# Attention block: values projected for four pairs of heads at a time, through DRAM, their bias added at the split of the output

## What is computed

```python
hn = (h - mu) * rsqrt(var + 1e-05) * gamma + beta
q = (hn @ Wq + bq).reshape(b, s, 16, 64)
k = (hn @ Wk + bk).reshape(b, s, 16, 64)
v = (hn @ Wv + bv).reshape(b, s, 16, 64)
q, k = _rope(q), _rope(k)
attn = softmax(where(tril, einsum('bihd,bjhd->bhij', q, k) / 8, -inf))
out = einsum('bhij,bjhd->bihd', attn, v).reshape(b, s, 1024)
x = _layernorm(h + out @ Wo + bo + h)
x = _layernorm(x + x + ffn(x))
```

## Time and profile before

| | |
|---|---|
| Time, median of 3 runs | 2310.25 us (2309.42 to 2313.67) |
| Profiled execution | 2305.9 us, span 2304.1 us |
| Granted TensorE clock, mean | 0.973 of full speed |
| Busy: TensorE, VectorE, ScalarE, GpSimd | 2144.3, 1691.7, 958.2, 1435.4 us |
| Attention pairs | from 71.5 us to about 1977 us |
| Transfers | 100.45 MB, 44 GB/s on average |

### The profile page before, as it was taken

The page is one execution under the profiler, slowest core; times in us unless marked ns, Lnnn a source line. Parts: engine busy times, 40 slices in busy tenths (PEclk is TensorE's granted clock), DMA queues, the critical chain, the costliest instruction groups (busy, mean ns, idle before and its releaser), DMA issues.

```text
span 2304.1 us, 43543 instructions
## 1 busy us (share of the span) xinstructions
PE 2144.3 (93%) x15872; PEld 1407.3 (61%) x15872; DVE 1691.7 (73%) x2318; ACT 958.2 (42%) x1301; POOL 1435.4 (62%) x1204
## 2 busy tenths in 40 slices
PE   5779999999999999899999999999999999889997
PEld 4446565556565656455656565556565654789996
DVE  8567878787878787777877777787777775466654
ACT  3334444444434443434444444444344445333433
POOL 2447777777777777566868686878687779200000
PEclk8799999999999999989999999999999999899999
DMA  5100101010101011101111111111111130222200
GB/s 161 63 22 19 46 19 46 21 43 22 42 24 41 24 41 54 48 19 32 33 32 33 32 33 33 33 32 33 33 29 36 29 115 10 96 92 73 100 19 28
DMA packets 79484, 100.45 MB, mean 44 GB/s; under 512 B 13984, under 2 KB 43680, under 8 KB 79008
## 3 DMA queue, kind: packets, MB, share of 16 engines
q1 hardware_dynamic: 79264, 97.60, 14.2%
HBM read 40.93 MB, written 23.07 MB: 28 GB/s over the span
## 4 chain that ended last, share of the span: by engine, by line
PE 73%; DVE 17%; issue 6%; ACT 1%; DMA 1%; SPq 1%; POOL 1%; DVEq 0%; ACTq 0%
PE o_ps L1150 17%; PE m_ps L1098 8%; DVE mpart L748 6%; PE x_ps L1053 6%; PE s_ps L1119 4%; PE x_ps L1055 4%; PE x_ps L1054 4%; PE s_ps L1121 4%; PE s_ps L1125 4%; PE s_ps L1123 4%; PE gu_ps L1053 2%; PE gu_ps L1054 2%; PE gu_ps L1055 2%; PE x_ps L1157 1%; DVE rot L787 1%
## 5 line engine op out<-in xcount | busy, mean ns | idle before, releaser
L474 POOL TENSOR_TENSOR acc<-acc,pt 128x512 f32<-128x512 f32 (+3 forms) x1024 | 1235.4, 1238 | 232.6 <-ACT pt L533 232.0
L748 DVE TENSOR_REDUCE mpart<-m_ps 128x2 f32<-128x1024 f32 (+2 forms) x576 | 625.6, 1086 | 342.1 <-PE m_ps L1098 205.5
L533 ACT ACTIVATE pt<-s_ps 128x1024 f32<-128x1024 f32 (+3 forms) x640 | 545.1, 896 | 561.7 <-PE s_ps L1125 319.5
L1150 PE MATMUL o_ps<-pt,v 128*64 128x512 f32 (+3 forms) x2560 | 555.4, 556 | 0.0
L1098 PE MATMUL m_ps<-qk 64*128 64x512 f32 (+3 forms) x1280 | 285.8, 442 | 102.5 <-DVE mpart L748 85.1
L1098 PEld LDWEIGHTS m_ps<-qk 64*128 64x128 f32 x1280 | 121.8, 186 | 384.0 <-issue 217.3
L1150 PEld LDWEIGHTS o_ps<-pt,v 128*64 128x64 f32 x2560 | 158.5, 139 | 232.5 <-issue 211.4
L469 POOL TENSOR_TENSOR acc<-pt 128x512 f32<-128x512 f32 (+1 forms) x128 | 165.5, 1313 | 200.0 <-ACT pt L533 200.0
L1119 PE MATMUL s_ps<-qk 64*128 64x512 f32 (+3 forms) x1280 | 249.8, 385 | 0.0
L1121 PE MATMUL s_ps<-qk 64*128 64x512 f32 (+3 forms) x1280 | 235.9, 363 | 0.0
L1125 PE MATMUL s_ps<-aux,ones_r 64*128 64x512 f32 (+3 forms) x1280 | 235.8, 362 | 0.0
(11 more groups left out here) (161 smaller groups left out, 3406.7 us busy)
## 6 DMA issues: line engine op xcount, KB each, us to landing
rot<-qr SPq DMA_DIRECT2D x512, 64.0 KB, 2.0
attn<-o_n SPq DMA_DIRECT2D x64, 256.0 KB, 2.1
o_raw<-attn SPq DMA_DIRECT2D x8, 2048.0 KB, 9.0
w_raw<-in_wqkv SPq DMA_DIRECT2D x51, 128.0 KB, 2.6
h_g<-in_h SPq DMA_DIRECT2D x8, 512.0 KB, 3.6
out<-out_g SPq DMA_DIRECT2D x7, 512.0 KB, 2.9
qk_place<-in_h SPq DMA_DIRECT2D x4, 512.0 KB, 5.8
pt<-in_h SPq DMA_DIRECT2D x4, 512.0 KB, 10.6
```

The costliest lines, as they stand in the source:

```text
L474: nc.gpsimd.tensor_tensor(sums, sums, probs, ALU.add).then_inc(summed, 1)
L533: nc.scalar.activation(pt[:, u % SLOTS, :, q0:NB], s_ps[:, two:two + 2, q0:NB], ACT.Exp, scale=SCALE)\
L748: nc.vector.tensor_reduce(dst, m_ps[:, :, 0:w], AX.X, ALU.max, negate=True).then_inc(maxed, 1)
L1150: last = nc.tensor.matmul(o_ps[rows, q0:NB], v[par][:, j, rows], pt[:, u % SLOTS, a, q0:NB], start=(j == 0), stop=(j == n - 1), skip_group ...
```

## The change

The values are no longer made for one pair of heads but for four (512 columns of Wv). One *piece* is a tile of 128 tokens: 6 matmuls with 512 columns into the bank. Four pairs need 16 pieces, and there are four such sets (two for each sequence). The first set is made in the opening; the second in pairs 0 to 3, four pieces in each, at the groups where the V chunks stood; the third, first of the second sequence, in pair 7, 16 pieces at `SWITCH_PLACES`, where a place (g, 1) is behind the weighing and sums of group g; the fourth in pairs 8 to 11, four in each. In pairs 4 to 6 and 12 to 15 none are made.

ScalarE copies a piece to `v_part`, SyncE stores it in `v_far` in DRAM (256 KB), and before each pair SyncE loads that pair's 128 columns into its `v` buffer: tiles 0 to 11 (768 KB) in group 1 of the pair before, tiles 12 to 15 (256 KB) in group 2 of the pair itself, both in runs of 512 bytes. For pair 8 the first load stands in group 14 of pair 7. The weights of four pairs, `wv_hl`, are loaded and split apart from those of Q and K, so the loads of `w_raw` per pair are two and not three.

The bias of the values is added where the attention output is split, from a column per partition. The loops of `each_pair` are written out. `o_n` and `r_b` are gone: the division is in place, and ScalarE's copy of the next `o_ps` waits for the store. The buffers of the last part stand in another order.

```diff
-VALUES = {g: int(x[1]) for g, x in XUSE.items() if x[0] == "V"}
+V_GROUPS = [g for g, x in XUSE.items() if x[0] == "V"]
+
+
+
+SWITCH_PLACES = [(3, 1), (4, 1), (5, 1), (7, 1), (8, 1), (9, 0), (9, 1), (10, 1), (11, 1), (13, 1), (14, 0), (14, 1),
+                 (15, 1), (16, 0), (16, 1), (17, 1)]
+V_PIECES = {it: {} for it in range(2 * PAIRS)}
+for it in range(4):
+    V_PIECES[it] = {(g, 0): (TT + 4 * it + i, 4 * it + i) for i, g in enumerate(V_GROUPS)}
+    V_PIECES[PAIRS + it] = {(g, 0): (3 * TT + 4 * it + i, 4 * it + i) for i, g in enumerate(V_GROUPS)}
+V_PIECES[PAIRS - 1] = {place: (2 * TT + i, i) for i, place in enumerate(SWITCH_PLACES)}
+
+WV_LOAD = {(0, 2): 2, (0, 5): 3, (5, 3): 4, (5, 6): 5, (8, 2): 6, (8, 5): 7}
+WV_SPLIT = {(0, 4): 2, (0, 7): 3, (5, 5): 4, (5, 8): 5, (8, 4): 6, (8, 7): 7}
+
...
-            pair(FIRST, 0, 0, 0, 0)
-            with engine.Fori(0, PAIRS // 2 - 1) as two:
-                pair(MIDDLE, two * 2 + 1, 1, two * 2 + 1, 0)
-                pair(MIDDLE, two * 2 + 2, 0, two * 2 + 2, 0)
-            pair(SWITCH, PAIRS - 1, 1, PAIRS - 1, 0)
-            pair(MIDDLE, PAIRS, 0, 0, 1)
-            with engine.Fori(0, PAIRS // 2 - 1) as two:
-                pair(MIDDLE, two * 2 + (PAIRS + 1), 1, two * 2 + 1, 1)
-                pair(MIDDLE, two * 2 + (PAIRS + 2), 0, two * 2 + 2, 1)
-            pair(LAST, 2 * PAIRS - 1, 1, PAIRS - 1, 1)
+            kinds = {0: FIRST, PAIRS - 1: SWITCH, 2 * PAIRS - 1: LAST}
+            for it in range(2 * PAIRS):
+                pair(kinds.get(it, MIDDLE), it, it % 2, it % PAIRS, it // PAIRS)
...
+            def load_v(it, c0, c1, done):
+
+                here, cols = slice(TG * c0, TG * c1), slice(it % 4 * P, (it % 4 + 1) * P)
+                sp.dma_start(v[it % 2][:, here, :], v_far[it // 4, here, :, cols].rearrange("t p n -> p t n"))\
+                  .then_inc(done, 16)
+
+            def store_v(it, place):
+                if place in V_PIECES[it]:
+                    n, t = V_PIECES[it][place]
+                    sp.wait_ge(v_done, n + 1)
+                    sp.dma_start(v_far[n // TT, t, :, :], v_part[:, :]).then_inc(v_stored, 16)
...
                 n0 = batch * SEQ + blk * NB
-                sp.dma_start(attn[bass.ds(head_rows, P), n0:n0 + NB], o_n[:, :]).then_inc(o_stored, 16)
+                sp.dma_start(attn[bass.ds(head_rows, P), n0:n0 + NB], o_sum[:, :]).then_inc(o_stored, 16)
...
                     if g in PIECE and kind is not LAST:
                         swap_halves(it + 1, *PIECE[g])
+                    store_v(it, (g, 0))
+                    store_v(it, (g, 1))
+                    if kind is SWITCH and g == 14:
+                        sp.wait_ge(v_stored, 16 * v_stored_for(it + 1, 2))
+                        load_v(it + 1, 0, 3, v_in)
+                    if (it, g) in WV_LOAD:
+                        sp.wait_ge(wv_lo, WV_LOAD[it, g])
+                        load_wv(WV_LOAD[it, g], wv_raw[:, :])
+                    if g == 2:
+                        if v_stored_for(it, 3) > 0:
+                            sp.wait_ge(v_stored, 16 * v_stored_for(it, 3))
+                        load_v(it, 3, 4, v_in3)
...
+                    if g == 1 and kind is not LAST:
+                        sp.wait_ge(pv_done, max(it * NG, 1))
+                        if kind is not SWITCH:
+                            if v_stored_for(it + 1, 2) > 0:
+                                sp.wait_ge(v_stored, 16 * v_stored_for(it + 1, 2))
+                            load_v(it + 1, 0, 3, v_in)
...
+                for t in range(TG * c, TG * (c + 1)):
+                    sp.wait_ge(v_done, t + 1)
+                    sp.dma_start(v_far[0, t, :, :], v_parts[t % 4]).then_inc(v_put[t % 4], 16)
...
+                if c == 0:
+                    for done in v_put:
+                        sp.wait_ge(done, 16 * BLOCKS)
+                    load_v(0, 0, 3, v_in)
...
             def evict_o(n, blk):
                 act.wait_ge(pv_done, n * NG + (BLOCK_ENDS[blk] + 1))
-                act.wait_ge(normed, n * BLOCKS + (blk + 1))
+                act.wait_ge(o_stored, (n * BLOCKS + blk) * 16 + 16)
                 nc.scalar.activation(o_sum[:, :], o_ps[:, :], ACT.Copy).then_inc(o_out, 1)
...
+            def evict_v(n, bank, dst):
+                act.wait_ge(v_proj, n + 1)
+                nc.scalar.activation(dst, bank, ACT.Copy).then_inc(v_done, 1)
+
+            def evict_v_first(c):
+                for t in range(TG * c, TG * (c + 1)):
+                    if t >= 4:
+                        act.wait_ge(v_put[t % 4], 16 * (t // 4))
+                    evict_v(t, v_bank[t % 2], v_parts[t % 4])
+
+            def evict_v_piece(it, place):
+                if place in V_PIECES[it]:
+                    n = V_PIECES[it][place][0]
+                    if n > TT:
+                        act.wait_ge(v_stored, 16 * (n - TT))
+                    evict_v(n, x_ps[:, :], v_part[:, :])
...
+                    evict_v_piece(it, (g - 1, 1))
...
-            def values(n, c, par, i):
-                dve.wait_ge(v_proj, n * BLOCKS + (c + 1))
-                if c == 0:
-                    dve.wait_ge(b_in, n * 32 + 32)
-                if c == 0 and i == 2:
-                    dve.wait_ge(pv_done, n * NG - NG)
-                nc.vector.tensor_tensor(v[par][:, TG * c:TG * (c + 1), :],
-                                        v_bank[i].rearrange("p (t n) -> p t n", t=TG),
-                                        b_v[:, par, :].unsqueeze(1).broadcast_to([P, TG, P]), ALU.add)\
-                  .then_inc(v_done, 1)
+            def rest_wv(n, raw):
+                dve.wait_ge(wv_hi, n + 1)
+                nc.vector.tensor_tensor(wv_hl[:, 1, n % KC, :], raw, wv_hl[:, 0, n % KC, :].bitcast(F32),
+                                        ALU.subtract).then_inc(wv_lo, 1)
...
             def divide(n, blk):
                 dve.wait_ge(r_back, n * BLOCKS + (blk + 1))
                 dve.wait_ge(o_out, n * BLOCKS + (blk + 1))
-                dve.wait_ge(o_stored, (n * BLOCKS + blk) * 16 + 16)
-                nc.vector.tensor_tensor(o_n[:, :], o_sum[:, :], r_b[:, :], ALU.mult).then_inc(normed, 1)
+                nc.vector.tensor_tensor(o_sum[:, :], o_sum[:, :], r_t[:, :], ALU.mult).then_inc(normed, 1)
...
-            def project_v(n, c, i):
-                for t in range(TG):
-                    here = slice(NB * c + P * t, NB * c + P * (t + 1))
-                    for k in range(KC):
-                        last = product(v_bank[i][:, t * P:(t + 1) * P], [hn[:, x, k, here] for x in range(2)],
-                                       [w_hl[:, x, k, 2 * P:3 * P] for x in range(2)],
-                                       first=(k == 0), last=(k == KC - 1))
+            def project_v(n, t, bank):
+
+                pe.wait_ge(wv_lo, KC * (n // TT + 1))
+                here = slice(P * t, P * (t + 1))
+                for k in range(KC):
+                    last = product(bank, [hn[:, x, k, here] for x in range(2)], [wv_hl[:, x, k, :] for x in range(2)],
+                                   first=(k == 0), last=(k == KC - 1))
                 last.then_inc(v_proj, 1)
...
                     if j == 0:
-                        pe.wait_ge(v_done, it * BLOCKS + (blk + 1))
+                        if blk == 0:
+                            pe.wait_ge(v_in, 16 * (it + 1))
+                        if blk == BLOCKS - 1:
+                            pe.wait_ge(v_in3, 16 * (it + 1))
...
-                def shared_free(g):
-
-                    for before in range(g - 1, -2, -1):
-                        x = XUSE[before % NG]
-                        n, i = (it if before >= 0 else it - 1), int(x[1])
-                        if x[0] in "QKV" and nxt:
-                            if x[0] == "V":
-                                pe.wait_ge(v_done, n * BLOCKS + (BLOCKS + i + 1))
-                            else:
-                                pe.wait_ge(cos_done, n * (2 * BLOCKS) + (2 * BLOCKS + 2 * i + "QK".index(x[0]) + 1))
+                def shared_free(g, behind):
+
+
+                    for place in range(2 * (NG * it + g) + behind - 1, -1, -1):
+                        n, b, late = place // (2 * NG), place // 2 % NG, place % 2
+                        if (b, late) in V_PIECES[n]:
+                            pe.wait_ge(v_done, V_PIECES[n][b, late][0] + 1)
                             return
-                        if x[0] == "M":
-                            own = n if before % NG < NG - 1 else n + 1
-                            pe.wait_ge(aux_done, own * BLOCKS + (i + 1))
+                        if late and b in SUMMED and (n, b) != (0, 0):
+                            pe.wait_ge(r_turned, (n - 1 if b == 0 else n) * BLOCKS + (SUMMED[b] + 1))
                             return
-                        if x[0] == "R" and (before > 0 or kind is not FIRST):
-                            own = n if before > 0 else n - 1
```

(25 more changed lines are left out.)

## The result

| | before | after |
|---|---|---|
| median | 2310.91 us (4 runs, 2309.42 to 2313.67) | 2294.75 us (4 runs, 2291.1 to 2298.65) |
| profiled execution, its span | 2305.9, 2304.1 us | 2298.65, 2296.9 us |

The ratio after to before is 0.9929 (95% interval 0.991 to 0.9948): faster by 16 us (0.7%), where 60 were forecast, and 4.75 us above the upper end of the range, 2290. The two profiled executions lie 7.25 us apart, since the one of before is 5 us under its median and the one of after is the slowest of its four.

What follows compares the result with a forecast made beforehand. TensorE's own instructions were taken as the bound (busy 93% of the span). Terms -50 - 31.5 - 2 + 2 + 19 + 4 - 8.5 + 7 gave -60 us: 2250 us as a median, range 2220 to 2290.

Steps and rivals of the forecast that it cites:

- I charge 3 us of new waits to a pair without V: Pairs 4 to 6, 12 to 14: 11.3 us of chunks gone, 3 us of TensorE waits added; six times 8.3, 50 less.
- Rival 2: VectorE, coupled with GpSimd, takes over; pairs without V gain 4 us, four-piece pairs 2.5; 2290 us; chance 0.18.
- Rival 1: TensorE stays the only bound; waits charged to relieved pairs and pair 7 vanish; 2223 us; chance 0.13.
- Rival 3: Q0's and K0's half swaps queue behind the value loads, slower than before; 2347 us at 100 GB/s; chance 0.05.
- 4 us for transfers: Value and weight loads ahead of Q0's half swaps delay them: 0.3 us a pair, 4 us more in all.
- Rival 4: Bank x_ps chains pieces everywhere, TensorE waiting for ScalarE's copy or a store; 2281 us; chance 0.06.
- Four-piece pairs: Pairs 1 to 3 and 8 to 11: 4.5 us less each, 31.5 in all; pairs 1 to 3 at 111 to 112.
- Pair 7: Switch of batches, 16 pieces for 4 chunks: 13.7 us of matmuls plus 5 of bank waits, 19 more (12 to 27).
- Splits of the V weights: VectorE's added splits in pairs 5 and 8, beside TensorE: 1 us each, 2 us more.
- The opening and pair 0: Opening: 16 pieces for 4 chunks, half hidden, 7 us more (3 to 14); pair 0: net 2 us less.
- Loops: Pairs 1 to 6 and 9 to 14 written out, no jumps: 8.5 us less (4 to 13).
- Pair 15 and the rest: Pair 15 had no V chunks and has no pieces; eviction, bias, stores and output copy were priced at nothing.

Runs made afterwards that it cites:

- short_rope: Changed kernel with VectorE's sine product, sum and remainder cut from 512 to 32 columns in pairs 4 to 6 and 12 to 14, output wrong: 2241.19 us.
- loops_out: Kernel before, with only the loops over pairs 1 to 6 and 9 to 14 written out: 2304.45 us, ratio 0.997 to before.
- fill6: Changed kernel plus six unread 512-column matmuls at each former V chunk place in pairs 4 to 6 and 12 to 14: 2280.52 us.
- fill24: Changed kernel plus 24 unread 128-column matmuls at each former V chunk place in pairs 4 to 6 and 12 to 14: 2304.51 us.
- two_pairs: Changed kernel with values made for two pairs at a time, eight pieces of two tiles by 256 columns a set: 2280.39 us.
- p7_moved: Changed kernel with pair 7's pieces moved from straight behind K0 and K1, and pair 8's first value load in group 18: 2293.52 us.
- two_spread: Against values made for two pairs at a time: second split-weight buffer, splits in groups 10 and 11, pair 7's row splits in eight halves: 2252.86 us.

## Why the prediction was wrong, step by step

**The step that failed** is "I charge 3 us of new waits to a pair without V". Held against short_rope, the waits cost 11.6 us in pair 13: 6.6 us of idle time and 5.0 us of the matmuls' own time at a lower granted clock. The term stood in the sum as -50 us for six pairs; the six pairs fell by 7.8 us in the traces (-5.4 and -2.4), of which loops_out has 2.3 (350.8 to 348.9 and 348.6 to 348.2), so the chunks gave 5.5, or 0.9 a pair, and what was charged at 3 us came to 10.4 on average. That is 44.5 us too few. Between the two traces the kernel fell by 7.2 us where 60 were forecast, a miss of 52.8; the other terms missed by 8.3 together, by errors of up to 9 us in both directions that follow below. (Between the medians the miss is 44.75 us. That this is nearly the 44.5 of the step is chance, since the execution profiled before lies 5.0 us under its median and the one after 3.9 above.) The bound was wrong too: I put the least gain of such a pair at 4 us, and it was 0.9.

Two readings led there. First, I took "TensorE busy 33.94 of 34 us" as proof that a microsecond of matmuls there is one of the pair. It says only that TensorE doesn't wait; that it had been filled to the point where VectorE comes ready is seen in the order of time, where the maxima start 0.05 us behind the reduction. Second, I compared VectorE's busy share over a block (84 to 88%), while the wait is set between two reductions, where three 512-column operations stand in a row. The sum to make was that of VectorE's instructions between two reductions against TensorE's between the two maxima.

**The clock** was in no term. The earlier trace rows had it: 0.91 in pair 0 and 0.94 in pair 7, where TensorE waits, 0.99 in pair 8, where it hardly does.

**Rival 2** gave 2290, the nearest number, and its sign came: the relieved pairs stayed above 112 us, with TensorE's idle time at the reductions. Its reason holds by half: VectorE does set the length of these pairs, but at single places and together with TensorE's clock, and not by being full. It had pairs with four pieces gain 2.5 us; they gained 4.4 (27.6 us in pairs 1 to 3 and 9 to 11, less 1.1 that loops_out has). And with VectorE alone as the bound fill6 could not have gained. **Rival 1** is excluded by fill24. **Rival 3**: VectorE's whole wait for swapped halves is 7.7 us (8.9 before), where I had said near 9, and a swap lands in 2.0 us as before; so no run shows anything of the 4 us for transfers. **Rival 4**: outside pair 7 TensorE shows no wait for the bank.

**Four-piece pairs**: forecast 111 to 112 us, found 110.9 to 112.4, with 113.5 in pair 9. A piece of pair 2, from its first matmul on:

```profile
407.73 0.50 PE L1147 MATMUL x_ps<-wv_hl,hn 128*128 128x512 f32 x1
408.06 0.39 PE L1148 MATMUL x_ps<-wv_hl,hn 128*128 128x512 f32 x1
...
408.99 0.40 PE L1149 MATMUL x_ps<-wv_hl,hn 128*128 128x512 f32 x1
```

Six starts in 1.26 us, the next work 0.3 later: the 1.56 us of the sum.

**Pair 7**: forecast +19 (12 to 27), found +24.6. The waits behind K0 and K1 were forecast at 4.2 us and came as 4.30 and 4.65. TensorE's idle time rose from 13.7 to 19.0 us, by the 5 that were charged; its busy time rose by 19.3 us, where the pieces less the chunks were priced at 13.7, and that is the 5.6 us missed. The granted clock fell from 0.94 to 0.90. With these two waits away the pair is at 149.9.

**Splits of the V weights**: +1 us each in pairs 5 and 8. Pair 8 was forecast 3.5 us shorter and is 2.1 longer: 5.6 us more, for two splits. TensorE is idle for 8.0 us of it (3.0 before), at a clock of 0.97. I had priced VectorE's instruction at 1 us (it took 1.30 and 1.43 here) and left out its wait for ScalarE's half, 2.23 and 1.67 us here and 2.26 in two_pairs.

**The opening and pair 0**: forecast +7 and -2, found -1.9 and -1.8 (from 71.53 to 69.61 us at the start of pair 0, and the rest up to R3). Pair 0 did not start near 78 but earlier than before:

```profile
43.47 23.05 POOL L513 TENSOR_SCALAR pt<-pt,mv,rstd 128x256 f32<-128x256 f32 x16 [43.03 <-DVE rstd L819]
...
69.61 0.50 PE L1192 MATMUL m_ps<-qk 64*128 64x512 f32 x2 [1.06 <-ACT qk_place L686]
```

GpSimd's rows start 1.6 us earlier than in the earlier trace rows, and the pair follows their end by 3.1 us (3.6 before); the sixteen evictions and 13.7 us of matmuls fit beside them. No run took this apart.

**Loops**: 8.5 us forecast, 6.6 measured between the medians, 3.4 between the pairs of the two profiles. **Pair 15 and the rest** were forecast unchanged and are 3.0 and 2.2 us longer in this profile; over the other kernels pair 15 lies between 104.8 and 108.8, so I put no cause to it.

## What to carry to other kernels

A busy share of 100% on the bounding engine does not say that its work has a price. Where two engines hand banks to each other, measure the slack at the handover: how long before the consumer's start the producer's end lies, and which instructions stand between two handovers on each. Work at a place with no slack is cover for the other engine; take it out evenly over such places, or move what it covered, and place a split where its engine waits anyway and behind, not beside, the half that it needs.

## What the runs showed of the hardware

In these runs TensorE paid twice for a longer wait, and the second price was partly chance. In the profiles of the changed kernel, fill6, p7_moved and two_spread I took every idle time of TensorE of 0.5 us or more between 222 and 1960 us, and the granted clock of the 4 us behind it. It was below 0.95, mostly at 0.57 to 0.7, as follows (the bounds are those of my table, not of the chip):

```
idle before    cases  clock fell
0.5 to 1.4 us    159           0
1.4 to 1.5 us     49          28
1.5 to 2.5 us     55          38
2.5 to 3.3 us     12          11
over 3.3 us       17          17
```

One place shows both: a wait in the middle of pair 2, of 1.43 us up to 358.21 us in the changed kernel and of 1.45 up to 359.47 in p7_moved, with the same instructions around it. The 4 us behind it, in the one and the other:

```profile
358.21:362.21 4.00, 4.00 (x26) 2.20 (x28) 3.42 (x5) 1.23 (x2) 1.29 (x3) 1.00 0.01 4
```

```profile
359.47:363.47 4.00, 4.00 (x14) 1.67 (x14) 3.12 (x4) 1.23 (x2) 1.27 (x3) 0.57 0.01 4
```

In the second row 14 matmuls stand where the first has 26. A pair with a mean clock of 0.98 is 1.4 to 1.6 us longer than an equal one at 1.00 (112.5 against 110.9 us in p7_moved), which is the step by which equal pairs differ in one execution. The Trainium skill, in "TensorE: Matmul & The Clock Gate", Part 1, puts it the other way about: the lower clock is the default, and activity releases it. The rows agree as far as they go: the clock fell behind idle time, and in pair 12 the idle time filled by fill6 (from 9.5 to 4.0 us) raised the mean clock from 0.96 to 0.98. Matmuls that nobody reads, put into the gaps, made a pair 2.4 us shorter.

VectorE's operations with both inputs in SBUF (sine product, sum, remainder, split) took 0.68 us at one place and up to 1.79 at another in the same kernel; the cosine product, with one input in PSUM, took 0.74 or 0.75 us in all 120 cases. The split took 1.25 us in group 4 (two_pairs) and 0.68 in group 11 (two_spread). What GpSimd did goes with it: in the trace of the changed kernel, the 80 sine products, sums and remainders that started while no instruction ran on GpSimd took 0.68 or 0.69 us each, and the 304 others up to 1.79. At the place of V0 above GpSimd was running when each of the three started. The Trainium skill, in "SBUF — State Buffer", section "SBUF: two separate sides", says that an operation of VectorE with two SBUF inputs and one of GpSimd that reads SBUF exclude each other: whichever starts first keeps the shared ports for its whole instruction. The rows fit that, but no run here held GpSimd still, so the cause was not shown.
